# A mixture-of-experts prologue in a new order: first products ahead of the merges, merges in threes

## The reference, cut to what matters

```
# conditioning, batch b with its expert e = itok_B_0_7[b]
h  = relu(x wi^T + 2 (x A_common) B_common + 2 (x A_e) B_e)       # 128 -> 512
y  = h wo^T + 2 (h A'_common) B'_common + 2 (h A'_e) B'_e         # 512 -> 128
# four rounds of a mixture of 4 experts, top 2 of them weighed by softmax
for r in range(4):
    logits = y Wg[r] + bg[r]; cw = weights of the two largest
    y = y + sum_e cw[e] * (gelu(y W1[e] + b1[e]) W2[e] + b2[e])
x = x + y
```

## Time and profile before

| what | us |
|---|---|
| median of 3 runs (lowest, highest) | 482.44 (481.11, 483.73) |
| the profiled execution's own time | 480.89 |
| its span, first to last instruction | 479.1 |
| TensorE busy in the span | 474.2 (99%) |
| DVE busy | 386.7 (81%) |
| ScalarE busy | 394.1 (82%) |
| POOL busy | 121.8 (25%) |

### The profile page before, as it was taken

The page is one execution under the profiler, slowest core; times in us unless marked ns, Lnnn a source line. Parts: engine busy times, 40 slices in busy tenths (PEclk is TensorE's granted clock), DMA queues, the critical chain, the costliest instruction groups (busy, mean ns, idle before and its releaser), DMA issues.

```text
span 479.1 us, 7437 instructions
## 1 busy us (share of the span) xinstructions
PE 474.2 (99%) x2260; PEld 394.7 (82%) x2260; DVE 386.7 (81%) x638; ACT 394.1 (82%) x543; POOL 121.8 (25%) x102
## 2 busy tenths in 40 slices
PE   8999999999999999999999999999999999999997
PEld 7998888888888888888888888888888888888886
DVE  4898999999889898988889898889896758654343
ACT  4889888887889898888888798898888888697644
POOL 4995212121211212122212121171314144500000
PEclk9999999999999999999999999999999999999999
DMA  8604702021120202020202112120202000000002
GB/s 225 201 24 133 286 1 90 1 90 34 57 88 0 88 0 88 0 88 0 88 1 88 43 45 88 45 90 0 88 2 88 2 0 0 1 1 0 0 23 69
DMA packets 8299, 27.03 MB, mean 56 GB/s; under 512 B 2258, under 2 KB 3602, under 8 KB 6098
## 3 DMA queue, kind: packets, MB, share of 16 engines
q1 hardware_dynamic: 7090, 22.45, 13.5%
q0 software_dynamic: 288, 2.88, 1.7%
q10 hardware_dynamic: 896, 1.38, 1.1%
HBM read 25.26 MB, written 1.44 MB: 56 GB/s over the span
## 4 chain that ended last, share of the span: by engine, by line
PE 98%; DMA 1%; SPq 0%; DVE 0%; issue 0%
PE bank L538 34%; PE bank L541 34%; PE bank L544 26%; PE bank L565 1%; PE bank L638 1%; PE bank L639 1%; PE bank L599 1%; DMA stage<-lora_all 1%; PE bank L562 0%; PE bank L634 0%; DVE x L1312 0%; SPq L251 0%; SPq L356 0%; SPq L355 0%; SPq L354 0%
## 5 line engine op out<-in xcount | busy, mean ns | idle before, releaser
L859 ACT ACTIVATE act_out<-bank,vec 128x512 f32<-128x512 f32 x256 | 165.1, 683 | 40.0 <-PE bank L544 27.9
L1154 DVE TENSOR_TENSOR hid_lo<-act_out,hid_hi 128x1024 fp32r<-128x1024 f32 x128 | 157.5, 1249 | 32.8 <-ACT hid_hi L864 32.7
L864 ACT ACTIVATE hid_hi<-act_out 128x1024 fp32r<-128x1024 f32 x128 | 136.2, 1064 | 8.2 <-ACT act_out L859 0.4
L502 POOL TENSOR_TENSOR cur<-cur,prod 128x512 f32<-128x512 f32 x48 | 65.8, 1370 | 232.5 <-DVE prod L1165 232.1
L538 PE MATMUL bank<-hid_hi,moe_hi 128*128 128x512 f32 x256 | 99.8, 390 | 0.0
L544 PE MATMUL bank<-hid_hi,moe_lo 128*128 128x512 f32 x256 | 99.7, 390 | 0.0
L541 PE MATMUL bank<-hid_lo,moe_hi 128*128 128x512 f32 x256 | 99.7, 389 | 0.0
L538 PE MATMUL bank<-xhi,moe_hi 128*128 128x512 f32 x256 | 99.6, 389 | 0.0
L541 PE MATMUL bank<-xlo,moe_hi 128*128 128x512 f32 x256 | 99.6, 389 | 0.0
L544 PE MATMUL bank<-xhi,moe_lo 128*128 128x512 f32 x256 | 99.6, 389 | 0.0
L538 PEld LDWEIGHTS bank<-hid_hi,moe_hi 128*128 128x128 f32 x256 | 48.1, 188 | 11.0
(11 more groups left out here) (134 smaller groups left out, 568.8 us busy)
## 6 DMA issues: line engine op xcount, KB each, us to landing
cw_all<-cw_dram SPq DMA_DIRECT2D x16, 1024.0 KB, 4.7
stage<-ffn_w POOLq DMA_DIRECT2D x1, 2304.0 KB, 8.7
cw_all<-moe_w SPq DMA_DIRECT2D x4, 512.0 KB, 7.2
stage<-lora_all SPq DMA_DIRECT2D x5, 160.0 KB, 4.5
x<-x_t SPq DMA_DIRECT2D x3, 256.0 KB, 5.2
out_t<-x SPq DMA_DIRECT2D x3, 256.0 KB, 2.4
cur<-cond_base ACTq DMA_DIRECT2D x2, 256.0 KB, 3.6
stage<-ffn_w POOLq DMA_DIRECT2D x1, 512.0 KB, 4.0
```

The source lines that it names most:

```text
L502: pool.tensor_tensor(cur[:, c, :], cur[:, c, :], prod[:, s % 2, :], ALU.add).then_inc(add_done, 1)
L859: act.activation(act_out[:, f // 2, f % 2, :], bank[:, f, :], ACT.Gelu_apprx_tanh, bias=vec[:, V_B1 + e * FC + f:V_B1 + e * FC + f + 1]).t ...
L864: act.activation(hid_hi[:, s % 2, 2 * pr:2 * pr + 2, :], act_out[:, pr, :, :], ACT.Copy)\
L1154: dve.tensor_tensor(hid_lo[:, s % 2, 2 * pr:2 * pr + 2, :], act_out[:, pr, :, :], hid_hi[:, s % 2, 2 * pr:2 * pr + 2, :].bitcast(F32), ALU ...
```

## The change

Nothing is computed that was not before; only orders, groups and banks change.

- **Merge groups.** Six groups instead of seven: the first two pairs stay, then four groups of three. The last group puts two of its results into banks 0 and 1.
- **TensorE's order.** The first two batches' hidden products come directly behind the filler, before the third merge group, interleaved by parts (first_high, first_x_low, first_low replace first_hidden); cond_out(0) and cond_out(1) follow the third group; merges and batches alternate from there; cond_hidden(6) comes behind cond_out(5). The last merge group also waits for relu_low(4), and cond_hidden(6) for the last two groups' sums.
- **DVE, ScalarE and POOL** get new orders to match. The gate weights' split moves behind the first four sums. The low part of x's chunk 1 moves from POOL to DVE.
- **Loads.** The base's second part is issued ahead of the fourth batch's factors on ScalarE's queue.

```
 MERGE_GROUPS = (((0, 0), (1, 0)),
                 ((0, 1), (1, 1)),
-                ((2, 0), (3, 0)),
-                ((2, 1), (3, 1)),
-                ((4, 0), (5, 0), (4, 1)),
-                ((6, 0), (7, 0), (5, 1)),
-                ((6, 1), (7, 1)))
+                ((2, 0), (3, 0), (2, 1)),
+                ((4, 0), (5, 0), (3, 1)),
+                ((6, 0), (4, 1), (5, 1)),
+                ((7, 0), (6, 1), (7, 1)))
-MERGE_BANKS = (6, 7, 2, 3, 5, 4, 6, 7, 4, 6, 7, 4, 6, 7, 4, 6)
+MERGE_BANKS = (6, 7, 4, 5, 6, 7, 4, 6, 7, 4, 4, 6, 7, 4, 0, 1)
...
@@ TensorE: merge_group
                 if last:
                     free = max(free, summed_in(LANG, first))
                     pe.wait_ge(lang_in, 16)
+                    pe.wait_ge(relu_lo, 5)
@@ TensorE: first_hidden(b) goes, its three parts stand alone
+            def first_high(b):
+                pe.wait_ge(mer_hi_done, HIGHS.index((b, 0)) + 1)
+                first_part(b, mer_hi[:, b, 0, :], xhi, start=True)
+            def first_x_low(b):
+                pe.wait_ge(x0_split[0], 1)
+                first_part(b, mer_hi[:, b, 0, :], xlo)
+            def first_low(b):
+                pe.wait_ge(mer_lo_done, LOWS.index((b, 0)) + 1)
+                first_part(b, mer_lo[:, b, 0, :], xhi, stop=True).then_inc(cond_h_done, 1)
             def cond_hidden(b):
...
+                if b == 6:
+                    pe.wait_ge(merge_free, max(summed_in(i, len(MERGED)) for i in range(2)))
@@ TensorE's order (before, then after)
-merge_group 0, 1, warm, merge_group 2, 3, first_hidden 0, 1, merge_group 4, cond_out 0, cond_hidden 2, merge_group 5, cond_out 1, cond_hidden 3, 4, merge_group 6, cond_out 2, 3, first_logits 0, cond_hidden 5, 6, cond_out 4, 5, first_logits 1, cond_hidden 7, expert_in (quarters 0, 1), cond_out 6, expert_in (2), cond_out 7, expert_in (3)
+merge_group 0, 1, warm, first_high 0, first_x_low 0, first_high 1, first_low 0, first_x_low 1, first_low 1, merge_group 2, cond_out 0, 1, cond_hidden 2, merge_group 3, cond_hidden 3, cond_out 2, cond_hidden 4, merge_group 4, cond_out 3, first_logits 0, cond_hidden 5, merge_group 5, cond_out 4, 5, cond_hidden 6, first_logits 1, cond_hidden 7, expert_in (0, 1), cond_out 6, expert_in (2), cond_out 7, expert_in (3)
@@ ScalarE's order after (merged_high and relu_high are mh, rh)
+base_load 1 ahead of lora_load 3; x0_high 0, mh(0,0), mh(1,0), mh(0,1), rh 0, mh(1,1), rh 1, mh(2,0), x0_high 1, x0_high 2, conditioned_high 0, mh(3,0), conditioned_copy 0, mh(2,1), rh 2, mh(4,0), rh 3, mh(3,1), mh(5,0), x0_high 3, moe_high 0, rh 4, mh(4,1), moe_high 4, conditioned_high 1, mh(5,1), conditioned_copy 1, mh(6,0), rh 5, lang_copy, mh(7,0), mh(6,1), moe_high 1, conditioned_high 2, conditioned_copy 2, mh(7,1), rh 6, moe_high 5, moe_high 2, rh 7
@@ DVE's order after (merged_sum is s)
+s(0,0), x0_low 0, s(1,0), s(0,1), s(1,1), split_gate, relu_low 0, s(2,0), relu_low 1, x0_low 1, s(3,0), s(2,1), x0_low 2, conditioned_low 0, s(4,0), relu_low 2, s(3,1), s(5,0), relu_low 3, x0_low 3, s(6,0), s(4,1), s(5,1), relu_low 4, conditioned_low 1, s(7,0), relu_low 5, s(6,1), s(7,1), gate_logits 0, gate_order 0, conditioned_low 2, relu_low 6, gate_choice 0, gate_gap 0, relu_low 7
@@ POOL's order after (merged_low is ml; x0_low 1 is gone from it)
+ml(0,0), ml(1,0), ml(0,1), ml(1,1), ml(2,0), ml(3,0), ml(2,1), ml(4,0), ml(3,1), ml(5,0), moe_low 0, ml(4,1), ml(5,1), ml(6,0), moe_low 4, ml(7,0), ml(6,1), ml(7,1), moe_low 1, ...
```

More of the change, by code:

```diff
@@ L459, in _ @@
             merged_low(0, 1)
-            x0_low(1)
+            merged_low(1, 1)
             merged_low(2, 0)
-            merged_low(1, 1)
             merged_low(3, 0)
@@ L465, in _ @@
             merged_low(4, 0)
-            merged_low(4, 1)
             merged_low(3, 1)
@@ L721, in _ @@
             warm(KEEP_WARM)
+            first_high(0)
+            first_x_low(0)
+            first_high(1)
+            first_low(0)
+            first_x_low(1)
+            first_low(1)
             merge_group(2)
+            cond_out(0)
+            cond_out(1)
+            cond_hidden(2)
             merge_group(3)
-            first_hidden(0)
-            first_hidden(1)
+            cond_hidden(3)
+            cond_out(2)
+            cond_hidden(4)
             merge_group(4)
[L727 to L734, removed]
             cond_out(3)
@@ L737, in _ @@
             cond_hidden(5)
-            cond_hidden(6)
+            merge_group(5)
             cond_out(4)
             cond_out(5)
+            cond_hidden(6)
             first_logits(1)
@@ L949, in _ @@
             first_load(act, 1)
+            base_load(act, 1)
             lora_load(act, 3)
-            base_load(act, 1)
             x0_high(0)
@@ L955, in _ @@
             merged_high(0, 1)
+            relu_high(0)
             merged_high(1, 1)
+            relu_high(1)
+            merged_high(2, 0)
             x0_high(1)
-            relu_high(0)
-            merged_high(2, 0)
+            x0_high(2)
+            conditioned_high(0)
+            merged_high(3, 0)
+            conditioned_copy(0)
             merged_high(2, 1)
+            relu_high(2)
+            merged_high(4, 0)
+            relu_high(3)
             merged_high(3, 1)
[L962 to L969, removed]
+            merged_high(5, 0)
             x0_high(3)
             moe_high(0)
-            relu_high(3)
-            merged_high(5, 0)
+            relu_high(4)
+            merged_high(4, 1)
             moe_high(4)
+            conditioned_high(1)
+            merged_high(5, 1)
+            conditioned_copy(1)
             merged_high(6, 0)
[L976 to L981, removed]
             relu_high(5)
             lang_copy()
+            merged_high(7, 0)
+            merged_high(6, 1)
             moe_high(1)
[L985 to L988, removed]
             conditioned_high(2)
             conditioned_copy(2)
+            merged_high(7, 1)
+            relu_high(6)
+            moe_high(5)
+            moe_high(2)
             relu_high(7)
@@ L1250, in relu_low @@
                    .then_inc(relu_lo, 1)
-            split_gate()
+            merged_sum(0, 0)
             x0_low(0)
-            merged_sum(0, 0)
             merged_sum(1, 0)
@@ L1257, in _ @@
             merged_sum(1, 1)
+            split_gate()
+            relu_low(0)
             merged_sum(2, 0)
+            relu_low(1)
+            x0_low(1)
             merged_sum(3, 0)
             merged_sum(2, 1)
+            x0_low(2)
+            conditioned_low(0)
+            merged_sum(4, 0)
+            relu_low(2)
             merged_sum(3, 1)
-            relu_low(0)
-            merged_sum(4, 0)
-            merged_sum(4, 1)
             merged_sum(5, 0)
-            relu_low(1)
-            x0_low(2)
-            relu_low(2)
-            merged_sum(7, 0)
-            merged_sum(6, 0)
-            merged_sum(5, 1)
-            conditioned_low(0)
             relu_low(3)
             x0_low(3)
+            merged_sum(6, 0)
+            merged_sum(4, 1)
+            merged_sum(5, 1)
+            relu_low(4)
+            conditioned_low(1)
+            merged_sum(7, 0)
+            relu_low(5)
             merged_sum(6, 1)
             merged_sum(7, 1)
-            relu_low(4)
-            conditioned_low(1)
             gate_logits(0, 0)
-            relu_low(5)
             gate_order(0, 0)
+            conditioned_low(2)
             relu_low(6)
             gate_choice(0, 0)
-            conditioned_low(2)
             gate_gap(0, 0)
```

41 lines of the change are left out of this document (14 added, 27 removed).

## The result

The changed kernel takes **487.24 us** (median of 6 runs, 486.19 to 488.32), the kernel before, run beside it, 481.84 (6 runs, 480.67 to 484.58). The ratio is **1.0113, with a 95% interval from 1.0090 to 1.0136**: slower by some 5.4 us, where 3.1 were forecast. The profiled execution after took 487.23 us around a span of 485.5.

What follows compares the result with a forecast made beforehand. TensorE, busy 99% of the span, was taken as the bound, so prologue losses arrive at the end. First product at 8.57 + 31.4 work + 0.2 gaps + 3.45 waits = 43.6 us for 40.53: +3.1, 485.5 us, range 483.3 to 487.5.

Steps and rivals of the forecast that it cites:

- the order: nine waits: TensorE in the prologue waits nine times in the new order, 3.45 us in sum; total +3.1 us, chance 0.63.
- split_gate late: On DVE, the moved gate split, 0.9 us, falls into idle time from 10.1 to 12.0 and costs nothing.
- The clock's fall: Rival: nine idle bits lower TensorE's clock, 36 products between 13.3 and 18.0 us cost 4.3 us more; 489.8 us, chance 0.05.
- The small gaps: On TensorE in the prologue, gaps ahead of merges: 0.2 us of before's 0.6 us beyond the bare sum counted as staying.
- The walk's loop product at 43.6: TensorE's first loop product near 43.6 us, where the kernel before had 40.53; a sign that the prediction is right.
- the bare sum: TensorE's prologue work from the first product or third merge group to the loop, priced without waits: 31.4 us.
- The missing cover at the first expert quarter: At expert_in, relu_low(6) has 1.9 us of cover where before had 4.8; TensorE waits 1.15 us.
- No wait in the loop: 0: Behind the prologue the gate's chain shifts 2.6 us, less than TensorE: 0, with up to 0.5 us for a late mixture.
- base_load and lora_load, swapped at 0: On ScalarE's load queue, base_load(1) comes 0.6 us earlier and lora_load(3) 0.6 us later; cost 0.
- The two waits added for banks 0 and 1: The last merges' wait for relu_low(4) and cond_hidden(6)'s for the last sum: 0.2 to 0.3 us of cover, no cost.
- Absorbed: Rival for the prologue: waits of 0.2 to 0.4 us vanish, +1.5 us remains, 483.9 us; chance 0.27.
- faster: Rival for the prologue: the chain through POOL never ends last, before's 0.6 us of gaps can go, 481.8 us; chance 0.05.

Runs made afterwards that it cites:

- experiment 1: The changed kernel with split_gate back at the head of DVE's order, ahead of the first merged_sum: 484.89 us, ratio 1.0067 to the kernel before.
- 5: The changed kernel with four filler products on the blank tile ahead of cond_out(0), split_gate still late: 486.54 us, ratio 1.0105 to the kernel before.
- experiment 3: The kernel before with only split_gate moved, behind DVE's first four sums: 487.37 us, ratio 1.0110.
- experiment 2: The changed kernel with split_gate moved later on DVE, behind x0_low(2): 488.05 us, ratio 1.0113 to the kernel before.
- 4: The changed kernel with nine filler products on the blank tile ahead of cond_out(0), split_gate still late: 486.44 us, ratio 1.0086 to the kernel before.
- 6: The changed kernel with split_gate first on DVE and x0_low(1) back on POOL: 485.51 us, ratio 1.0081 to the kernel before.
- 8: The changed kernel, split_gate first, cond_hidden(6) ahead of cond_out(5), POOL's blank write ahead of the last six moe_low: 484.60 us, ratio 1.0069 to before.
- 7: The changed kernel, split_gate first, cond_hidden(6) ahead of cond_out(5), relus of 6 and 7 earlier to match: 486.07 us, ratio 1.0108 to before.
- experiment 9: The kernel before with only the base's second part issued ahead of lora_load(3): 482.18 us, ratio 1.0008.

## Why the prediction was right and wrong

Slower was right, with 487.24 inside the range, near its upper end. That it is inside is in part luck: 3.1 us were forecast and 5.4 measured, and 5.4 on top of the 482.44 that the forecast started from would be 487.8, above the range; beside the changed kernel the kernel before ran 0.6 us faster. And the upper part of the range was meant for the loop and for scatter, not for the 1.7 and 1.2 us that filled it. The profiles split the 41.09 - 34.65 = 6.4 us like this:

| part | forecast | measured |
|---|---|---|
| the order: nine waits | 3.1 | 3.5 (1 less before) |
| split_gate late | 0 | 1.7 (5 less 1) |
| the clock's fall | 0 (a rival at 0.05) | 1.2 (after less 5) |

- **The nine waits.** Right in their sum and most of them in size, as experiment 1 shows with the gate split out of the way; only the two walked at cond_hidden(3) and cond_out(2) came nearly whole at the second. By the spacing of starts (a block over 1.43 us, a merge group over 1.18):

| wait | walked | measured in 1 |
|---|---|---|
| first_high(1) | 0.26 | 0.25 |
| cond_out(0) | 0.39 | 0.36 |
| cond_out(1) | 0.29 | 0.34 |
| cond_hidden(2) | 0.06 | 0.08 |
| cond_hidden(3) | 0.33 | 0.07 |
| cond_out(2) | 0.18 | 0.40 |
| cond_out(4) | 0.27 | 0.28 |
| cond_out(5) | 0.52 | 0.47 |
| expert_in, first quarter | 1.15 | 1.23 |
| sum | 3.45 | 3.48 |

- **The small gaps were sized too low.** The walk's loop product at 43.6 is measured at 43.96, with a first merge 0.1 earlier, and the waits aren't the reason. What is left of TensorE's time after the bare sum (31.3 us with 1.18 for a merge group) and the waits, 0.05 to 0.10 us at most changes from one block to the next, comes to 0.7 us in experiment 1 (35.51 from first_high(0)) and, with waits and all, to 0.7 in before (40.53 - 8.50 = 32.03): it stays, where the prediction counted 0.2 us as staying and took the rest of before's 0.6 for waiting that could be won. That is the 0.4 us between 3.1 and 3.5. ScalarE idles 1.35 us ahead of merged_high(4, 1) in after (1.5 forecast).
- **The step that failed** is "split_gate, 0.9 us of DVE, falls into DVE's idle time from 10.1 to 12.0". DVE was idle in that stretch, but POOL wasn't, and the 0.9 us were the price beside an idle POOL (its queue begins at 8.55). I had charged x0_low for meeting POOL in the very same walk, from rows of 1.20 for 0.69, and didn't ask it of the small copies. The runs show 3.7 us in place of the 0.9, and a cond_out(0) that is 1.7 us later for it.
- **The clock.** The mechanism of the rival was right and its size too large: priced at 36 products and 4.3 us, it touched 15 or 16, some 15 x (0.213 - 0.119) = 1.4 us locally, 1.2 net. What was wrong was the reason: I took nine short idle bits as the cause, and those of experiment 1, up to 1.08 us of idle, leave the clock at 1.00. The other argument, a clock of 1.00 over the idle time ahead of 5.88 us, was weak: in before that column reads 1.00 from the first product on, while its first 20 records take 4.13 us. In the trace of after what stands ahead of the fall is the one gap of 2.13 us, which the failed step had made. A fall does not need such a kernel in every execution, nor does such a kernel always bring one: a mean clock of 0.996 or less stands in 5 of 6 executions of after, 3 of 4 of experiment 3 and 1 of 4 of experiment 2, in none of the 24 of experiments 1, 4, 5, 6 and 8, but once each in 7 (of 4), in 9 (of 10) and in the kernel before. What those three executions had ahead of the fall no kept trace shows.
- **The missing cover at the first expert quarter** was named and sized rightly, but experiments 7 and 8 show that it isn't worth what it waits: of the 1.3 and 1.2 us won, 1.5 and 1.0 came back as waits in the loop. "No wait in the loop: 0" holds for the change (438.8 us behind the loop's start for 438.6); that it holds because the change reaches the loop late is what 7 and 8 suggest, which reach it earlier and lose time there (440.4 and 440.0).
- **base_load and lora_load, swapped at 0**: right in the changed kernel, where no merge waits for factors; in experiment 9, without the cover named, a merge group waits 0.95 us for its factors, though only part of that is shown to come from the swap. The two waits added for banks 0 and 1 kept their cover: in experiment 1 the last merges start at 28.83, 0.21 us behind the last product's start, and cond_hidden(6) at 33.69, 1.50 us behind cond_out(5)'s.
- **Absorbed and faster** fell: with the gate split out of the way the order still costs 3.5 us, where they had 1.5 and under 0. The waits of 0.2 to 0.4 us did not vanish.

None of the versions beats the kernel before: its prologue holds almost no idle time (34.61 us busy of 34.65, the filler of 1.2 us behind the first merges among it, which the change keeps), and the small gaps stayed in both orders. A new order could win little without removing work, and this one removes none.

## What to carry to other kernels

Before you move a small operation into an idle stretch of its engine, look at what the neighbour that shares its ports does in that stretch: a copy of 16 columns cost up to 1.24 us under POOL and 0.17 with POOL idle. Read a wait from the spacing of starts where records overlap. A wait that grows on an otherwise dense TensorE can have a second price, the products behind it at the lower clock. And when the bottleneck is 99% busy, an order that brings consumers forward must show, wait by wait, that every producer still has its cover.

## What the runs showed of the hardware

- DVE operations of 128x16 to 128x128 took 0.17 to 0.23 us with POOL idle and 1.01 to 1.27 us when they started inside a POOL subtraction, each ending within 0.1 us of it (after, experiments 2 and 3). Sums that read one operand from PSUM stayed at 0.68 us with POOL busy. A subtraction of 128x1024 with both operands in SBUF took 1.23 us with POOL idle and 1.21 to 1.92 with it busy (7 and 8).
- In the profiled executions the granted clock fell after one TensorE idle of 2.13, 2.43 or 3.44 us (after, 2, 3); it didn't after one of 1.05 (5), 1.08 (1) or 1.23 (7), each between busy stretches.
- At the head of a trace the clock column says 1.00 while the products run slowly: 20 records of filler in 4.53 us against 8 in 1.16 later (after), and a first merge group at half pace in 2 and 4.
- A gap that the profile puts down to "issue" was a wait for another engine: cond_out(0) starts 0.10 us after the end of DVE's relu_low(0) both in after (14.77, 14.87) and in experiment 1 (13.20, 13.30).
